# Maxima transposed between the halves of the value products, query and key projection right behind them

## The reference

```
for c in range(6):                       # nodes
    q = ew[c,0] * (nodes[in_q] @ We[eq] + be[eq])
    k = ew[c,1] * (nodes[in_k] @ We[ek] + be[ek])
    v = ew[c,2] * (nodes[in_v] @ We[ev] + be[ev])
    o = mha(q, k, v, Wq[c], Wk[c], Wv[c], Wo[c])   # 8 heads of width 16, softmax over 256 keys
    nodes[c] = act_w[c] * o + q
out = layernorm(nodes[5])
```

## Time and profile before

| | us |
|---|---|
| median of 3 runs | 1070.54 (1068.91 to 1070.84) |
| profiled execution, its own time | 1071.46 |
| its span | 1069.7 |
| TensorE busy (matmul) | 995.8 (93%) |
| VectorE busy | 837.9 (78%) |
| ScalarE busy | 730.5 (68%) |
| GpSimd busy | 447.4 (42%) |

### The profile page before, as it was taken

The page is one execution under the profiler, slowest core; times in us unless marked ns, Lnnn a source line. Parts: engine busy times, 40 slices in busy tenths (PEclk is TensorE's granted clock), DMA queues, the critical chain, the costliest instruction groups (busy, mean ns, idle before and its releaser), DMA issues.

```text
span 1069.7 us, 26895 instructions
## 1 busy us (share of the span) xinstructions
PE 995.8 (93%) x9705; PEld 704.7 (66%) x9705; DVE 837.9 (78%) x1805; ACT 730.5 (68%) x1601; POOL 447.4 (42%) x874
## 2 busy tenths in 40 slices
PE   8989999998899999999999999999999999999995
PEld 4755655655566776776767777767666766776663
DVE  5466777766689988887887899888788878878895
ACT  3345666664577777777777778877777777777775
POOL 3522232233333343334444358843433344443365
PEclk9889999999899999999999999999999999999998
DMA  8100000006476667667676776677676667766651
GB/s 226 34 1 1 1 0 0 0 2 89 70 104 97 95 92 107 101 97 103 96 105 93 105 104 109 115 112 102 91 106 101 98 100 103 100 92 105 102 75 33
DMA packets 84695, 87.33 MB, mean 82 GB/s; under 512 B 11642, under 2 KB 70526, under 8 KB 84574
## 3 DMA queue, kind: packets, MB, share of 16 engines
q1 hardware_dynamic: 82974, 83.69, 51.7%
q0 software_dynamic: 800, 1.98, 0.9%
q10 hardware_dynamic: 800, 0.05, 0.0%
HBM read 6.90 MB, written 2.10 MB: 8 GB/s over the span
## 4 chain that ended last, share of the span: by engine, by line
PE 48%; DMA 17%; DVE 12%; SPq 9%; issue 5%; ACT 5%; POOL 3%; DVEq 0%; POOLq 0%; ACTq 0%
PE bank L1289 46%; DMA mst<-mrows 17%; SPq L502 6%; DVE region L1155 3%; SPq L516 2%; POOL hl L592 2%; ACT region L817 1%; DVE region L1087 1%; DVE region L971 1%; DVE region L1082 1%; PE bank L1625 1%; ACT region L793 1%; DVE region L1075 1%; DVE region L1036 1%; POOL hl L589 0%
## 5 line engine op out<-in xcount | busy, mean ns | idle before, releaser
L1155 DVE TENSOR_REDUCE region<-bank 128x2 f32<-128x512 f32 x768 | 488.9, 680 | 124.5 <-PE bank L1289 118.5
L817 ACT ACTIVATE region<-bank 128x512 f32<-128x512 f32 x768 | 409.7, 609 | 60.6 <-PE bank L1289 60.6
L1289 PE MATMUL bank<-st 48*128 48x256 f32 x3072 | 325.0, 330 | 5.6 <-DVE region L1155 4.2
L1289 PEld LDWEIGHTS bank<-st 48*128 48x128 f32 x3072 | 250.7, 189 | 28.0 <-DVE region L1155 4.7
L589 POOL TENSOR_TENSOR hl<-qk,one_col 128x512 fp32r<-128x512 f32 x96 | 100.1, 1043 | 400.1 <-ACT qk L782 400.1
L1289 PE MATMUL bank<-region 128*32 128x256 f32 (+3 forms) x3554 | 250.0, 377 | 2.2 <-DVE region L1182 1.2
L1289 PEld LDWEIGHTS bank<-region 128*32 128x32 f32 (+2 forms) x3554 | 130.9, 117 | 85.4 <-issue 16.6
L1289 PE MATMUL bank<-mst,ones 64*128 64x512 bf16 x768 | 151.3, 387 | 27.5 <-DMA mst<-mrows 25.1
L592 POOL TENSOR_TENSOR hl<-qk,hl 128x512 fp32r<-128x512 f32 x96 | 122.6, 1277 | 7.5
L839 ACT ACTIVATE mrows<-bank 24x256 bf16<-24x256 bf16 x96 | 35.8, 373 | 126.6 <-PE bank L1625 126.6
L1289 PEld LDWEIGHTS bank<-mst,ones 64*128 64x128 bf16 x768 | 37.2, 93 | 91.4 <-DMA mst<-mrows 40.4
(11 more groups left out here) (193 smaller groups left out, 1276.3 us busy)
## 6 DMA issues: line engine op xcount, KB each, us to landing
st<-hl SPq DMA_DIRECT2D x576, 128.0 KB, 4.5
mst<-mrows SPq DMA_DIRECT2D x192, 6.0 KB
out<-xall POOLq DMA_DIRECT2D x14, 128.0 KB, 3.8
xall<-in_L_attn_hidden_states SPq DMA_DIRECT2D x1, 768.0 KB, 8.4
cst<-in_constants SPq DMA_DIRECT2D x1, 514.5 KB, 4.1
xT<-in_L_ffn_Wq SPq DMA_DIRECT2D x1, 384.0 KB
xT<-in_L_ffn_Wk SPq DMA_DIRECT2D x1, 384.0 KB
xT<-in_L_ffn_Wv SPq DMA_DIRECT2D x1, 384.0 KB
```

The source lines that it names most:

```text
L817: act.activation(to, x_bank(x, k, e)[:, :].rearrange("p (j q) -> p j q", j=2), ACT.Exp).then_inc(B["exp_ok"], 1)
L1155: dve.tensor_reduce(mx[s.n % 2][:, to:to + 2], s_bank(s, k, e)[:, :].rearrange("p (j k) -> p j k", j=2), AX_X, ALU.max, negate=True).then_ ...
L1289: return pe.matmul(o, w, x, start=start, stop=stop, skip_group_check=skip)
```

## The change

- The value products are issued in two halves of 16 matmuls (heads 0 to 3, heads 4 to 7), and the transposes of the maxima stand between them.
- The queries and keys are projected right behind the second half, ahead of x1, and ScalarE copies them ahead of exps 1. Before, they stood behind s2 and behind exps 2.
- The residual product moves ahead of x3 and s3; the output product stays behind s3. For the last node the two residual matmuls come first and then the two output matmuls, where before they took turns.
- The maxima rows go to `mst` by one DMA in place of two. They land on partitions 0, 24, 48, 72, 96 and 120, so still three in either half.

```diff
+MSTEP = 24
@@ SP, maxima_rows
-                for s in range(2):
-                    of = s * MROW * JH
-                    sp.dma_start(mst[m.n % 2][HALF * s:HALF * s + MROW, :, :], mrows[m.n % 2][of:of + MROW * JH, :]).then_inc(m_in[m.n % 2], 16)
+                sp.dma_start(mst[m.n % 2][0:(2 * MROW - 1) * MSTEP + 1:MSTEP, :, :], mrows[m.n % 2][:, :]).then_inc(m_in[m.n % 2], 16)
@@ ScalarE, phase (and in copy_rows, as in weights, 32 * uses becomes 16 * uses)
                 if m is not None:
                     copy_rows(m)
+                if a is not None:
+                    copy_qk(a)
                 if x is not None:
                     exps(x, 1)
 ...
                 if x is not None:
                     exps(x, 2)
-                if a is not None:
-                    copy_qk(a)
@@ TensorE
-            def pv(d):
+            def pv_ready(d):
                 (the waits of pv)
+            def pv_half(d, g):
+                for kt in range(KT):
+                    for j in range(GCOL):
+                        h = g * GCOL + j
+                        k = mm(bank[OUT][32 * j:32 * j + 32, g * T:(g + 1) * T], vaug[d.n % VALS][:, kt, VW * h:VW * h + VW],
+                               probT[d.n % 2][:, kt * H + h, :], start=(kt == 0), stop=(kt == KT - 1), skip=True)
+                if g == 1:
+                    k.then_inc(B["pv_ok"], 1)
+            def residual(d):
+                to, prev = bank[OUT], source(d, GRAPH[d.c]["src"][0])
                 pe.wait_ge(B["outT_ok"].sem, B["outT_ok"].at(d.n))
                 if not d.last:
                     mm(to[:, T:2 * T], w_res[:, d.c, :], prev, stop=False)
-                    pe.wait_ge(B["ctxT_ok"].sem, B["ctxT_ok"].at(d.n))
+                else:
+                    for t in range(KT):
+                        mm(to[:, T + t * P:T + (t + 1) * P], prev[:, t * P:(t + 1) * P], w_res[:, d.c, :], start=(t == 0), stop=False, skip=True)
+            def project(d):
+                to = bank[OUT]
+                pe.wait_ge(B["ctxT_ok"].sem, B["ctxT_ok"].at(d.n))
                 if not d.last:
                     mm(to[:, T:2 * T], w_out[:, d.c, :], ctxT, start=False).then_inc(B["node_ps"].sem, 1)
                 else:
                     (two matmuls by w_out, one for each 128 columns)
@@ TensorE, phase
                 if d is not None:
-                    pv(d)
+                    pv_ready(d)
+                    pv_half(d, 0)
 ...
                 if m is not None:
                     transpose_maxima(m)
+                if d is not None:
+                    pv_half(d, 1)
+                if a is not None:
+                    project_qk(a)
                 burst((1, 2), (2,))
                 if t in (EARLY, EARLY + 1):
                     warm(2, OUT)
-                if a is not None:
-                    project_qk(a)
+                if d is not None:
+                    residual(d)
                 burst((3,), (3,))
```

More of the change, by code:

```diff
@@ L837, in copy_rows @@
                 if old is not None:
-                    act.wait_ge(m_in[old.n % 2], 32 * old.uses(2))
+                    act.wait_ge(m_in[old.n % 2], 16 * old.uses(2))
                 act.activation(mrows[m.n % 2][:, :], bank[IN][0:MCOLS, 0:P].bitcast(BF16), ACT.Copy).then_inc(B["mt_ok"], 1)
@@ L1602, in weights @@
                 if k == 0:
-                    pe.wait_ge(m_in[x.n % 2], 32 * x.uses(2))
+                    pe.wait_ge(m_in[x.n % 2], 16 * x.uses(2))
                 for e in range(2):
@@ L1650, in project @@
                     mm(to[:, T:2 * T], w_res[:, d.c, :], prev, stop=False)
-                    pe.wait_ge(B["ctxT_ok"].sem, B["ctxT_ok"].at(d.n))
+                else:
[4 more added lines that the diff above has]
+                pe.wait_ge(B["ctxT_ok"].sem, B["ctxT_ok"].at(d.n))
+                if not d.last:
                     mm(to[:, T:2 * T], w_out[:, d.c, :], ctxT, start=False).then_inc(B["node_ps"].sem, 1)
                 else:
-                    pe.wait_ge(B["ctxT_ok"].sem, B["ctxT_ok"].at(d.n))
                     for t in range(KT):
-                        r, o = slice(t * P, (t + 1) * P), slice(T + t * P, T + (t + 1) * P)
-                        mm(to[:, o], prev[:, r], w_res[:, d.c, :], stop=False)
-                        k = mm(to[:, o], ctxT[:, r], w_out[:, d.c, :], start=False)
+                        k = mm(to[:, T + t * P:T + (t + 1) * P], ctxT[:, t * P:(t + 1) * P], w_out[:, d.c, :], start=False, skip=True)
                     k.then_inc(B["node_ps"].sem, 1)
```

## The result

| | before | changed |
|---|---|---|
| median | 1069.72 us (4 runs, 1068.23 to 1070.84) | 1109.14 us (4 runs, 1108.83 to 1109.81) |
| profiled execution, its span | 1071.46, 1069.7 | 1109.13, 1107.3 |
| mean of the 92 slots with queries | 8.17 us | 8.62 us |

The account below looks back on a forecast made before the run. TensorE's order of work was taken as the bound, with a small DMA wait. Terms 2.99 + 1.17 + 0.72 + 2.07 + 0.57 + 0.53 + 0.54 = 8.59 us a slot; 1071.5 + 38.6 - 1 = 1109, range 1088 to 1124.

Parts of the forecast that it names:

- the sum's main term: Slot with queries, x0 to x0: 8.59 us against 8.17 before, times 92 slots, +38.6 us.
- The DMA wait costs 0.37 a slot: TensorE ahead of x0, waiting for the maxima rows: 0.37 us a slot, 34 us in all, expected to go whole.
- Queries ahead of x1: Queries' matmuls to ScalarE's first copy 1.17 us, copy to exponentials 0.72; exps 1 start at 4.88 instead of 3.65.
- Exps 1 and 2 to the work behind s3: ScalarE's exps 1 and 2 take 2.07 us, then 0.57 to TensorE's work behind s3.
- Output product first behind s3: TensorE behind s3: charged 0.53 us, as the residual cost there, instead of 0.44 as the second product.
- Residual: Residual product ahead of x3: costs nothing, since TensorE would otherwise be idle there.
- The two gates: TensorE waits for ScalarE at x3 and s3: two idle gaps, about 1.2 of 8.59 us, some 0.4 ahead of x3.
- the 7.80: Kernel before: length in us of a slot at whose end nothing waits, x0 to x0.
- The value products in two halves: TensorE from x0 to the end of this block: same matmuls and transposes, 2.99 us as before.
- faster: Rival, 8%: s3 follows x3 without ScalarE, every slot 7.80 or a little less, 1037 us.
- Slower still: Rival, 5%: s3's maxima reach the transposes too late, TensorE waits in the middle of the value products, 1123 to 1137.
- The clock: Rival, 4%: TensorE busy 86% instead of 96%; a fall to 1.2 GHz in one slot of ten gives 1172.

Follow-up runs that it names:

- the first of these kernels: The kernel before, with the maxima rows in one transfer issued on GpSimd's queue in place of SP's, behind the split of the maxima: 1090.00 us, ratio 1.0186.

## Why the prediction was right

The forecast was 1109, the result is 1109.14, and the sum's main term is right to the hundredth: 8.59 us a slot forecast, 8.59 or 8.60 measured in 74 of the 92. I go through its steps.

**What bounded the kernel.** "The DMA wait costs 0.37 a slot" holds as the price of the wait. But I took the wait for something that an earlier transpose and one issue less would shorten, and it isn't: one transfer alone gave 0.9999, the queries back in place with both parts kept gave the full wait. What removed it is that the queries are copied 1.4 us earlier. From the start of that copy to the landing of the rows in the next slot it is 10.61 to 10.63 us at the median in each of the eleven kernels whose rows go by SP, wherever the copy, the transposes and the rows' own issue stand; the rows land when the stacking traffic of these queries is through. So with the copy c us into the slot a slot isn't shorter than (c + 10.63) / 2. With c = 5.57 that is 8.10 (8.17 measured, mostly between 7.8 and 8.6); with c = 4.15 it is 7.4, and with 4.71 it is 7.7. There the rows land 2.41 and 1.06 us ahead of x0 at the median, and no slot waits for them. I had put the landing in the changed kernel at 7.1 into the slot; it is at 6.18. The swing in the kernel before is the same loop: a short slot makes the next one's landing late against it.

**Queries ahead of x1**: 1.17 forecast, 1.17 measured; copies to exponentials 0.72, measured 0.73. **Exps 1 and 2 to the work behind s3**: 2.07 + 0.57, measured 617.23 - 614.60 = 2.63. **Output product first behind s3**: 0.53, measured 0.54, as in the row I used. The Trainium skill, page "TensorE: Matmul & The Clock Gate", section on what happens when a matmul is issued, lets TensorE load the next weights during the running matmul when the row groups don't conflict or the load goes to a background buffer. The 0.44 that I took from that rule did not come; no run here tells which of its conditions failed. **Residual**: free ahead of x3, shown by putting it back, +0.44 a slot.

**The two gates.** Here the size of the parts was off, though not their sum. In the kernel with the residual ahead alone nothing waits between the residual and the values:

```profile
605.68 0.59 PE L1288 MATMUL bank<-region,w_res 128*128 128x256 f32 x2
606.20 0.39 PE L1288 MATMUL bank<-mst,ones 64*128 64x512 bf16 x2
...
607.00 0.70 PE L1288 MATMUL bank<-region,w_out 128*128 128x256 f32 x2
```

It takes 0.52 from the residual to x3 and 0.80 from x3 to the output product. In the changed kernel it takes 0.63 and 1.58. So TensorE loses 0.1 us at x3 and 0.8 at s3, 0.9 in a slot, where I had forecast about 1.2 in all and some 0.4 at x3. In the kernel before, x3 to the work behind s3 takes 0.98: nearly 0.2 us of the 7.80 was the same gate, and the profile shows no idle time there.

**The value products in two halves** were costed at nothing with no gain named for them but the earlier transposes. The chain stayed at 2.98, so the cost was right; the gain was misplaced. It is the cover for the copy of the rows: without it 9.30.

**Small terms that cancelled.** The median fits better than the sum deserves. The slots average 8.62, not 8.59, which is 2.6 us over the 92: seven slots around the final scaling take some 0.16 more, as ScalarE's extra work delays the copy of the rows and with it the queries, and four slots with the last transposes of the first stage take 0.33 or 0.59 more. I had counted none of that. Against it stand 1.9 us ahead of the first x0, which I had not foreseen and no run explains (the first x0 comes between 270.9 and 276.7 in the kernels here), and 1.8 at the end, where I had put 1. That the total then meets the forecast within a microsecond is luck.

**The rivals.** The gate was real; the case "faster" falls with the 0.44 us ahead of s3. "Slower still", by late maxima, did not happen in the changed kernel: GpSimd's last part is ready at 611.26, 1.54 us into the slot, 0.37 ahead of the transposes. But walls of this kind stood close by. The transposes waited for GpSimd in three experiments (the copies back, the queries back, the transposes between the halves with GpSimd's queue), there because the queries' split stood in front and not because the maxima came late. And with the values ahead of s3 the maxima did come late, for the banks of s1. The clock stayed up:

```profile
280.00:1040.00 760.00, 719.74 (x7614) 507.43 (x7615) 601.67 (x1129) 538.69 (x1175) 322.58 (x633) 1.00 0.69 96
```

Granted 1.00, with TensorE busy for 719.74 of 760 us, 95%; I had said 86%. The record counts the modelled tail of a matmul as busy, so the 0.8 us at s3 show as 0.44 and the 0.1 at x3 as nothing. By starts alone TensorE works for 7.70 of 8.59 us, 90%. The swing that the Trainium skill, page "TensorE: Matmul & The Clock Gate", section on the second failure mode, describes was not seen.

## What to carry to other kernels

A pipelined slot is the longest of several loops that run across engines, and here five of them lie close together: TensorE's own work (7.6 us in the shortest slots), the exponentials that give s3 its banks (8.59 with the queries ahead), the stacking transfers up to the landing (8.10 with the queries in their old place), GpSimd's two splits in their order (8.19 with the transposes early as well), and the maxima that give s1 its banks. Before an instruction is moved forward on an in-order engine, write down for each loop what stands behind it until the next gate; a part that shortens one loop (the early residual, the single transfer) is worth nothing until that loop is the longest, and moving work out from behind a gate can uncover another wait. An instruction that comes forward can also lengthen a loop that runs through it: the early transposes put 0.87 us on the one through GpSimd. When a wait for a transfer is to go, ask first what is ahead of it in the DMA engines: here starting the big traffic earlier helped, and neither fewer issues nor another queue did.

## What was not expected of the hardware

A transfer of 12 KB from SBUF to SBUF, issued from GpSimd on a queue of its own, took 4.0 us to land at the median, 1.7 at best and 5.8 at worst, beside 768 KB of stacking traffic a slot (the share of the sixteen DMA engines was 1.08 to 1.22 in the three full microseconds shown). Issued from SP behind that traffic it landed no later: 10.63 us behind the copy of the queries at the median, and 10.79 from GpSimd.

A program whose GpSimd issues these 96 transfers ends with a drain of GpSimd of 9.4 us, 1.5 us where SP issues them. The span of the first of these kernels is longer by 7.1 us for it, though every output has landed.

SP needs 0.77 us for the issue of 24 rows in one transfer and 1.55 for two of 12.
